# Relative-bias attention in a four-layer kernel: heads projected one by one and divided where they are added to X

## The reference

```
q, k, v = shape(h @ Wq), shape(h @ Wk), shape(h @ Wv)   # h: layernorm(x); 16 heads x 64
scores  = einsum('bhqd,bhkd->bhqk', q, k) + position_bias   # bias depends on k - q alone
attn    = softmax(scores, axis=-1)
out     = einsum('bhqk,bhkd->bhqd', attn, v)
x       = x + concat_heads(out) @ Wo
```

## Time and profile before

| | |
|---|---|
| median of 3 runs | 5371.87 us (5360.46 to 5372.24) |
| profiled execution, its own time | 5377.29 us |
| span of the profiled execution | 5375.2 us |
| busy in the span | TensorE 84%, weight loads 41%, VectorE 62%, ScalarE 50%, GpSimd 36% |
| mean granted TensorE clock | 0.931 |

### The profile page before, as it was taken

How to read it: one execution, slowest core, us unless ns; L and a number is a source line. 1 busy time by engine, 2 the same in 40 slices (tenths; PEclk the granted TensorE clock), 3 DMA queues, 4 the chain that set the end, 5 groups by cost and what they waited for, 6 DMA issues and landing times. The chain is left out here.

```text
span 5375.2 us, 70831 instructions
## 1 busy us (share of the span) xinstructions
PE 4499.2 (84%) x22404; PEld 2208.3 (41%) x22502; DVE 3330.0 (62%) x7491; ACT 2666.8 (50%) x4966; POOL 1911.9 (36%) x2206
## 2 busy tenths in 40 slices
PE   4678887988879888898888988798887888889888
PEld 2134334443444434443344433454334443445344
DVE  5766755667556674666655666556765667464445
ACT  2255553556526554365543745445553556436453
POOL 2746520555106541175301852036520555110200
PEclk8889998999989999999989999899998999999789
DMA  3523210332104211042100421023210332101000
GB/s 126 158 72 110 76 53 1 105 96 71 41 3 136 79 61 35 3 161 65 57 28 25 159 63 53 13 67 116 75 50 5 100 99 71 40 3 56 1 28 7
DMA packets 166645, 345.29 MB, mean 64 GB/s; under 512 B 18000, under 2 KB 26704, under 8 KB 166240
## 3 DMA queue, kind: packets, MB, share of 16 engines
q1 hardware_dynamic: 166256, 340.54, 19.9%
HBM read 337.25 MB, written 3.21 MB: 63 GB/s over the span
## 5 line engine op out<-in xcount | busy, mean ns | idle before, releaser
L196 PE MATMUL BANKS<-WB 128*128 128x512 bf16 x1518 | 440.1, 439 | 191.1 <-DVE XN L441 45.0
L1939 ACT ACTIVATE heads_prob<-BANKS 128x512 f32<-128x512 f32 (+3 forms) x768 | 365.3, 519 | 193.3 <-PE BANKS L1834 188.8
L407 POOL TENSOR_TENSOR rstd<-rstd,WF 128x4 f32<-128x4 f32 x48 | 48.5, 1011 | 944.7 <-DVE rstd L428 944.7
L1207 DVE CUSTOM_DVE_ANT_0 attn_biased<-BANKS,attn_toep 128x512 f32<-128x512 f32 x384 | 257.8, 682 | 188.3 <-PE BANKS L1095 134.1
L782 POOL TENSOR_TENSOR heads_work<-heads_work,heads_c_all 128x512 f32<-128x512 f32 x192 | 243.7, 1270 | 293.6 <-DVE heads_work L817 293.0
L196 PEld LDWEIGHTS BANKS<-WB 128*128 128x128 bf16 x1616 | 168.8, 110 | 422.8 <-issue 215.4
L212 POOL TENSOR_TENSOR rstd<-rstd,WF 128x4 f32<-128x4 f32 x24 | 24.3, 1011 | 787.5 <-DVE rstd L230 787.5
L1304 PEld LDWEIGHTS BANKS<-last_x_w,last_x_a 128*128 128x128 f32 x1536 | 214.7, 205 | 175.1 <-ACT last_x_a L1344 91.7
L1977 DVE CUSTOM_DVE_ANT_0 BANKS<-BANKS,WF 128x384 f32<-128x384 f32 (+3 forms) x512 | 241.2, 510 | 70.4 <-PE BANKS L1834 67.8
L1304 PE MATMUL BANKS<-last_x_w,last_x_a 128*128 128x128 f32 x1536 | 222.3, 291 | 71.0 <-ACT last_x_a L1344 71.0
L1980 DVE TENSOR_REDUCE heads_nmax<-BANKS 128x1 f32<-128x512 f32 x384 | 244.2, 682 | 60.1 <-PE BANKS L1834 59.0
(11 more groups left out here) (913 smaller groups left out, 10921.5 us busy)
## 6 DMA issues: line engine op xcount, KB each, us to landing
heads_c_all<-bc_rows SPq DMA_DIRECT2D x192, 256.0 KB, 3.2
attn_toep<-bias_line SPq DMA_DIRECT2D x96, 448.0 KB, 4.6
XNM<-bc_rows SPq DMA_DIRECT2D x112, 256.0 KB, 3.1
XTM<-bc_rows SPq DMA_DIRECT2D x112, 256.0 KB, 3.5
XO<-bc_rows SPq DMA_DIRECT2D x112, 256.0 KB, 3.3
XN<-bc_rows SPq DMA_DIRECT2D x112, 256.0 KB, 3.2
heads_b_all<-bc_rows SPq DMA_DIRECT2D x96, 256.0 KB, 3.6
last_x_w<-in_w SPq DMA_DIRECT2D x48, 512.0 KB, 3.7
```

Of the source, the lines that this page charges most:

```text
L196: nc.tensor.matmul(bank, ident_b, bc(ident_b[:, 0:1], [P, SEQ]), start=True, stop=True)
L1207: V.tensor_tensor_reduce(biased[:, s % NS_, :], PS[s % NS_], toep[:, h % 4, c:c + SEQ], -1.0, BIG, ALU.add, ALU.min, nmax[:, s:s + 1]).the ...
L1939: nc.scalar.activation(prob[:, i % PR, lo:hi], bank("T", i)[:, lo:hi], ACT.Exp).then_inc(exped, 1)
```

## The change

- The reciprocals are no longer spread by products. Bank 5 is copied as it is to `ot` (now by ScalarE), each head is projected by itself (64 rows of the array, two banks), and VectorE multiplies each 128 by 128 piece by the reciprocal of its row's sum as it adds it to X: eight instructions per pair, four for each head.
- Keys and values are reversed over the whole sequence (`XT` is written backwards by the norm), and queries are turned back; the bias line is reversed to match, and no reversal is left to undo.
- The ring has three banks, the scores have three in place of four. `biased` keeps four buffers, `prob` has six in place of five.
- The scores of a pair of steps are issued one step earlier, in the odd step.

```diff
-        NS_, NP_, NT_ = 4, 5, 2 * PAIR
-        RING = (PS[4], PS[7])
+        NS_, NB_, NP_, NT_ = 3, 4, 6, 2 * PAIR
+        RING = (PS[3], PS[4], PS[7])
+        NR = len(RING)
...
-            if spread_in(s) is not None:
-                order.append(("spread", spread_in(s)))
             if projected_in(s) is not None:
-                order.append(("project", projected_in(s)))
+                order += [("project", projected_in(s), 0), ("project", projected_in(s), 1)]
...
             def project(p):
-                bank = ring(("project", p))
+                halves = [ring(("project", p, a)) for a in range(2)]
                 pe.wait_ge(emptied, p + 1)
                 for j in range(NJ):
-                    last = nc.tensor.matmul(bank[:, j * D:(j + 1) * D], ot[:, p % 2, j * P:(j + 1) * P],
-                                            W("Wo")[:, p * D:(p + 1) * D], start=True, stop=True)
-                last.then_inc(filled, 1)
+                    for a in range(2):
+                        rows = slice(DK * a, DK * (a + 1))
+                        last = nc.tensor.matmul(halves[a][:, j * D:(j + 1) * D], ot[rows, p % 2, j * P:(j + 1) * P],
+                                                W("Wo")[rows, p * D:(p + 1) * D], start=True, stop=True)
+                        if j == NJ - 1:
+                            last.then_inc(filled, 1)
+
+            def score(s):
+                r, j = unit(s)[:2]
+                if s % PAIR == 0:
+                    pe.wait_ge(*freed(("make", r, 1)))
+                if s >= NS_ - 1:
+                    pe.wait_ge(maxed, s - NS_ + 2)
...
             make(0, 1)
+            score(0)
             for s in range(LAST):
                 r, rest = s // PAIR, s % PAIR
-                if s < U and s % 2 == 0:
+                if s + 1 < U and s % 2 == 1:
                     yield at(s)
...
+                    score(s + 1)
...
-                    nc.scalar.copy(dst if i else dst[:, :, ::-1],
-                                   bank.rearrange("p (j t) -> p j t", j=NJ)).then_inc(made, 1)
+                    dst = qk[:, r % 2, i, :]
+                    nc.scalar.copy(dst if i else dst[:, ::-1], bank).then_inc(made, 1)
...
+            def empty(w):
+                act.wait_ge(weighed, w + 1)
+                if w >= 2:
+                    act.wait_ge(filled, place["project", w - 2, 1] + 1)
+                nc.scalar.copy(ot[:, w % 2, :], PS[5]).then_inc(emptied, 1)
...
-            def add(p):
-                n = place["project", p]
+            def add(p, a):
+                n = place["project", p, a]
                 dve.wait_ge(filled, n + 1)
-                if p:
-                    dve.wait_ge(summed, p)
-                V.tensor_tensor(X[:, :, :], X[:, :, :], RING[n % 2].rearrange(tiles, j=NJ), ALU.add).then_inc(summed, 1)
...
+                if a == 0:
+                    dve.wait_ge(inverted, p + 1)
+                for j in range(NJ):
+                    done = PAIR * p + NJ * a + j
+                    if done >= NJ:
+                        dve.wait_ge(summed, done - NJ + 1)
+                    u = PAIR * p + 2 * j + a
+                    V.scalar_tensor_tensor(X[:, j, :], RING[n % NR][:, j * D:(j + 1) * D], rden[:, u:u + 1], X[:, j, :],
+                                           ALU.mult, ALU.add).then_inc(summed, 1)
...
-                    c = P * (NJ - 1 - j)
+                    c = P * j
...
-            norm_tiles(st, "ln", X, XN, XT, beside=await_weights)
+            norm_tiles(st, "ln", X, XN, XT[:, ::-1], beside=await_weights)
...
-    rel = np.arange(1024) - (SEQ - 1)
+    rel = (SEQ - 1) - np.arange(1024)
```

More of the change, by code:

```diff
@@ L955, in attn1_parts @@
             st.sem(n) for n in ("filled", "made", "copied_a", "copied_v", "scored", "maxed", "exped", "inverted"))
-        weighed, emptied, summed, spread = (st.sem(n) for n in ("weighed", "emptied", "summed", "spread"))
-        SPREAD_AT = 5
+        weighed, emptied, summed = (st.sem(n) for n in ("weighed", "emptied", "summed"))
         def at(s):
@@ L1011, in freed @@
             if item[0] == "project":
-                return summed, item[1] + 1
-            if item[0] == "spread":
-                return spread, item[1] + 1
+                return summed, PAIR * item[1] + NJ * (item[2] + 1)
             u = item[1]
@@ L1029, in ring @@
                 n = place[item]
-                if n >= 2:
-                    pe.wait_ge(*freed(order[n - 2]))
-                return RING[n % 2]
+                if n >= NR:
+                    pe.wait_ge(*freed(order[n - NR]))
+                return RING[n % NR]
             def make(r, i):
@@ L1045, in project @@
             def project(p):
-                bank = ring(("project", p))
+                halves = [ring(("project", p, a)) for a in range(2)]
                 pe.wait_ge(emptied, p + 1)
                 for j in range(NJ):
-                    last = nc.tensor.matmul(bank[:, j * D:(j + 1) * D], ot[:, p % 2, j * P:(j + 1) * P],
-                                            W("Wo")[:, p * D:(p + 1) * D], start=True, stop=True)
-                last.then_inc(filled, 1)
-            def spread_out(w):
-                bank = ring(("spread", w))
-                pe.wait_ge(inverted, w + 1)
-                for a in range(2):
[L1057 to L1062, removed]
+                    for a in range(2):
[10 more added lines that the diff above has]
+                    pe.wait_ge(maxed, s - NS_ + 2)
+                for a in range(2):
+                    o = DK * a
+                    q, k = qk[o:o + DK, r % 2, 0, :], qk[o:o + DK, r % 2, 1, :]
+                    nc.tensor.matmul(PS[(s + a) % NS_], q[:, j * P:(j + 1) * P], k,
+                                     start=True, stop=True).then_inc(scored, 1)
             def weigh(w, kt):
@@ L1129, in move @@
                 act.wait_ge(filled, n + 1)
-                bank = RING[n % 2]
+                bank = RING[n % NR]
                 if i == 2:
@@ L1135, in move @@
                 else:
-                    dst = qk[:, r % 2, i, :].rearrange("p (j t) -> p j t", j=NJ)
-                    nc.scalar.copy(dst if i else dst[:, :, ::-1],
-                                   bank.rearrange("p (j t) -> p j t", j=NJ)).then_inc(made, 1)
[L1140 to L1145, removed]
+                    dst = qk[:, r % 2, i, :]
[5 more added lines that the diff above has]
+                nc.scalar.copy(ot[:, w % 2, :], PS[5]).then_inc(emptied, 1)
             yield -2.0
@@ L1156, in scalar @@
                         act.wait_ge(filled, place["turn", e - NP_] + 1)
-                    nc.scalar.activation(prob[:, e % NP_, :], biased[:, e % NS_, :], ACT.Exp, bias=nmax[:, e:e + 1],
+                    nc.scalar.activation(prob[:, e % NP_, :], biased[:, e % NB_, :], ACT.Exp, bias=nmax[:, e:e + 1],
                                          scale=-1.0, accum_out=den[:, e:e + 1]).then_inc(exped, 1)
@@ L1165, in scalar @@
                         act.wait_ge(weighed, (u - NT_) // PAIR + 1)
[L1166 to L1169, removed]
+                    nc.scalar.copy(probt[:, u % NT_, :], RING[n % NR]).then_inc(copied_a, 1)
+                w = s // PAIR - 2
+                if s % PAIR == EMPTY_AT and 0 <= w < NPAIR:
+                    yield at(s) + 1.4
+                    empty(w)
                 if made_in(s):
@@ L1172, in scalar @@
                     move(*made_in(s))
+            yield at(LAST) + 1.0
+            empty(NPAIR - 1)
         def gpsimd(pool):
@@ L1220, in vector @@
                         dve.wait_ge(weighed, (u - NT_) // PAIR + 1)
[L1221 to L1225 removed]
+                    V.tensor_copy(probt[:, u % NT_, :], RING[n % NR]).then_inc(copied_v, 1)
                 if projected_in(s) is not None:
                     yield at(s) + 1.7
[L1228 to L1230 removed]
+                    add(projected_in(s), 0)
+                if s and projected_in(s - 1) is not None:
+                    yield at(s) + 1.7
+                    add(projected_in(s - 1), 1)
             yield at(LAST) + 3.0
[L1232 removed]
+            add(NPAIR - 1, 0)
+            add(NPAIR - 1, 1)
         pieces = Pieces()
```

44 lines of the change are left out of this document (5 added, 39 removed).

## The result

The changed kernel takes 5282.99 us (median of 3 runs, 5277.45 to 5286.52) against 5371.87; the ratio is 0.984, 95% interval 0.982 to 0.985. A second measurement of it gave 5274.68. So it is faster, by 89 to 98 us, where 128 were forecast. The profiled execution is the one of 5282.99 us.

A forecast was written before the change was run, and what follows sets the result against it. TensorE was taken as the bound, with 8.3 us of waits beside a scan. Seven scanning stages at -17.6 us give -123, the bare one -5: -128 from 5377.3, so 5249, in medians 5244; range 5195 to 5303, about 0.85.

The forecast's parts named there:

- Spread removed, shape changes: TensorE, per attention stage: removed spread saves 9.5 us, extra full/half-array changes from moved scores cost 4.7; sum -4.8.
- Projection by head: TensorE: sixteen 64-row products overlap in two halves and take 0.89 us again, so no net cost.
- The rival of no overlap: TensorE projections: the array halves don't overlap, 57 us of the gain go back, 5301 us; chance 0.04.
- Emptying to ScalarE, tail: ScalarE swaps one copy for another, even; a scanning stage's tail falls from 17.0 to 10.0 us, -7.0.
- Small additions: VectorE: eight 128-column additions at 0.26 us, +0.9 per pair; nothing in the middle, full price in the tail.
- the rival's 58 us: VectorE becomes the bound by its small additions: 58 us of the gain go back, 5302 us; chance 0.06.
- Third ring bank: Scanning stages: with the emptying off VectorE, aimed at 8.3 us of TensorE waits, of which 2.5 are kept.
- Three score banks, scores a step ahead: Scores hang on the maximum of the pair just ahead; priced at nothing beyond the waits kept.
- the slower rival: Each score waits for a maximum queued behind a scan; at 1.0 us per pair 5461 us; chance 0.06.
- The waits-stay rival: Queues of VectorE and GpSimd merely move TensorE's waits; gain 88 us, 5284 us; chance 0.20.
- GpSimd as a floor: GpSimd's scan work sets a floor near 127.5 us for a scanning stage before its tail.
- The first stage taken for all seven: Scanning stages: first stage's -10.6 and tail's -7.0 make -17.6, taken seven times for -123 us.

The follow-up runs named there:

- the third bank alone: Kernel before the change, with a third ring bank taken from the scores, which keep three banks; all else as before: 5340.46 us, ratio 0.994.
- the kernel with the scores back: Changed kernel with the scores issued in the even step again, ahead of its transposes: 5242.98 us, ratio 0.976.
- the two-bank kernel: Changed kernel with two ring banks in place of three, three score banks kept: 5335.11 us, ratio 0.994.
- the scan behind: Changed kernel with each scan queued behind the even step's maximum instead of ahead of it, scores still a step ahead: 5242.94 us, ratio 0.977.
- the kernel with the halves in turn: Changed kernel with a projection's products ordered head by head instead of alternating: 5287.35 us, ratio 0.984.
- the one that has only the pause put back: Changed kernel where the tail's first weighing also waits for the scan's last result (L925), emptying still on ScalarE: 5298.50 us, ratio 0.986.
- the eight-column sums: Changed kernel with scores in the even step, GpSimd's sums cut from 512 to 8 columns, result incomplete: 5220.07 us against 5242.98.
- the rows first: Changed kernel with scores in the even step, bias rows of heads 2 and 3 loaded behind the scan's first rows: 5227.86 us, ratio 0.973.
- the kernel with two decays: Changed kernel with the decay alternating between its bank and an SBUF buffer, five probability buffers instead of six: 5323.27 us, ratio 0.991.

## Why the prediction was right in sign and short in size

*Spread removed, shape changes.* Forecast -9.5 and +4.7 us per stage. The bare stage came out at 127.2 for 128.0, but partly by luck, for errors cancel in it. The third ring bank alone takes 2.7 us off it (132.8 to 130.1), where the forecast had nothing: it read 110.52 busy of 110.88 as a stage without waits. The same product of a `make` in the kernel before and in that with the third bank alone:

```profile
4893.45 1.02 PE L1037 MATMUL BANKS<-XT,WF 128*128 128x512 f32 x2
4894.51 0.66 PE L1103 MATMUL BANKS<-WF,zattn_prob 128*128 128x128 f32 x4
```

```profile
4871.18 1.02 PE L1038 MATMUL BANKS<-XT,WF 128*128 128x512 f32 x2
4872.03 0.60 PE L1104 MATMUL BANKS<-WF,zattn_prob 128*128 128x128 f32 x4
```

It occupies 1.06 us, and 0.85 with the third bank, and is busy for 1.02 in both: a wait this short hides behind the recorded duration. From there to the kernel with the scores back, 130.1 to 124.5, it is -5.6. By the starts of the products, the spread and the weighings ahead of it give -9.4, as forecast; the projections take +1.2 and the transposes +2.5, of which 1.3 is one wait for an addition; the forecast had both at nothing. The scores a step ahead then cost +2.7 (124.5 to 127.2) for a forecast 4.7: 2.1 is TensorE's busy time, 0.07 per excursion for 31 and not 0.15, and 0.6 is waits for maxima.

*Projection by head.* Forecast 0.89, measured 0.99:

```profile
420.26 1.16 PE L1041 MATMUL BANKS<-WF,attn_ot 64*128 64x128 f32 x16
421.25 1.03 PE L1055 MATMUL BANKS<-attn_qk 64*128 64x512 f32 x4
```

The rival of no overlap is out: undoing the alternation makes a projection of the bare stage 1.44 where it took 1.01.

*Emptying to ScalarE, tail.* Forecast 17.0 to 10.0, to the end of the last addition; measured, to the next norm, 10.2 from 16.1 to 17.4. The emptying back on VectorE brings the old tail back (15.6 to 17.2): shown.

*Small additions.* Forecast 0.26 us each and at nothing in the middle. VectorE's rows in the changed kernel:

```profile
421.45 1.13 DVE L1175 SCALAR_TENSOR_TENSOR X<-BANKS,attn_rden,X 128x128 f32<-128x128 f32 x4
422.50 0.68 DVE L1189 CUSTOM_DVE_ANT_0 attn_biased<-BANKS,attn_toep 128x512 f32<-128x512 f32 x1
423.10 1.12 DVE L1175 SCALAR_TENSOR_TENSOR X<-BANKS,attn_rden,X 128x128 f32<-128x128 f32 x4
```

Four take 1.05 us of queue (421.45 to 422.50), 0.26 each, where one operation on 512 columns takes 0.60 (422.50 to 423.10). The Trainium skill (VectorE: DVE Perf Modes, The TRN2 errata) says small pieces pay a latency each time; the rows agree. In the bare stage and in the first scanning stage alike 1.7 us of TensorE's waits are put down to L1175: small, and not the rival's 58 us.

*Third ring bank.* Forecast: keep 2.5 us of the waits for copies and banks. None were kept. Right in kind; the two-bank kernel shows that 60 us hang on it, twice what the bank is worth on the kernel before (5372 to 5340), because the change itself makes the ring busier. The emptying off VectorE, which the forecast counted beside it, did nothing in the middle.

*Three score banks, scores a step ahead: the step that failed.* It was priced at nothing beyond the waits kept. It brings 6.4 us of waits for maxima in the first stage, 3.7 with the scores back and 1.5 with the scan behind; the scan's place alone takes 30 us off the kernel's attention. The mechanism had been named as the slower rival and set aside, because the maximum and the score need less than half of the 4.0 us between two scores. That compared their work with the interval, and left out the scan of 1.2 us ahead of them and the scan's own wait for its decay (up to 1.5 us). The maximum comes late in six of 31 pairs of steps, so the price was 0.2 us per pair and not the rival's 1.0. It did not show in the stage's sum, 135.4 for 134.4, because the forecast had kept 6.4 us of other waits (2.5 and 3.9), most of which went: two errors that nearly cancel. The waits-stay rival names 5284, where the time fell, and it said that the queues would move the waits. But it let a scanning stage gain 4.8 us, where 9.0 were measured, and its sign, waits ahead of transposes for copies, did not come; its sum agrees because of the microseconds outside attention.

*GpSimd as a floor.* Forecast 127.5 per stage. The best kernels stand at 129.5, and the sums' removal takes only 2 us off: near it, not on it.

*The first stage taken for all seven.* Attention fell by 114.8 us and not by 128. The step multiplied the first stage's numbers by seven: its tail of before was 17.4 us to the next norm, the others' 16.1 to 16.5, so the tails gave 6.3 on the mean and not 7.0; and the stages gave 9.0 and not 10.6, the seventh of after being 137.9. The last sequence gave 7.5 and not 5: 5.6 before its tail, and 1.8 ahead of its first scores, where the profiled execution before had a granted clock of 0.64 for 9.5 us and that of after 1.00 for 7.7.

*Outside attention: no step at all.* The other 26 us of the 39 that the forecast is short of 5282.99 lie here (rest 4035.8 before, 4061.7 after; 4054.4 in the second measurement). The same stretches behind the fifth attention, before and after:

```profile
3108.00:3123.60 15.60, 12.17 (x62) 8.28 (x65) 9.20 (x37) 1.25 (x4) 1.02 (x1) 0.89 0.00 1
3123.60:3215.30 91.70, 77.45 (x473) 30.53 (x476) 67.62 (x193) 58.51 (x124) 58.20 (x116) 0.98 0.29 84
```

```profile
3038.20:3054.00 15.80, 11.73 (x62) 7.19 (x65) 9.24 (x37) 1.26 (x4) 1.02 (x1) 0.85 0.00 1
3054.00:3147.10 93.10, 79.51 (x473) 31.46 (x476) 67.62 (x194) 58.63 (x124) 58.08 (x116) 0.95 0.26 83
```

The work is the same; the granted clock is 0.89 and 0.98 here with a pause of TensorE ahead, 0.85 and 0.95 without one. It need not be the pause, though. The same place in the kernel with the halves in turn, which has no pause:

```profile
3042.10:3058.60 16.50, 13.08 (x64) 7.58 (x65) 9.23 (x37) 1.25 (x4) 1.02 (x1) 0.82 0.00 1
3058.60:3148.90 90.30, 76.53 (x475) 30.50 (x476) 67.58 (x194) 58.52 (x124) 57.96 (x116) 1.00 0.27 85
```

Over the seven scanning sequences the two stretches sum to 754.9 us before and 769.6 after, but also to 753.6 in this kernel and 754.0 with two ring banks, both without the pause, and to 759.2 in the one that has only the pause put back. Two kernels put the pause back with the change otherwise in place, and both have their rest, by medians, at 4041, against 4050 to 4062 in most kernels without it. But the third bank on the kernel before has the pause and 4048.2, the eight-column sums have none and 4043.6, and one kernel repeats only within 7, or within 15 in its profiled executions. What costs the 19 to 26 us outside attention stays open; the runs show that the granted clock there changes with the kernel and the execution.

## What to carry to other kernels

When a wait is taken from one consumer of a busy in-order queue, ask who is next behind the same long instruction. Here the copies were freed of the scan and the scores tied to it; compare the chain in front of the new wait, the long instruction and its own wait included, with the slack, not the work alone. Nor does a busy share near 100% say that an engine never waits: on an engine at 110.52 of 110.88 us a third bank still found 2.7. Of two cures for one wait try each alone first: the scores back in their place and the scan moved gave over 30 us each, and with the rows first the second on top of the first gave nothing (5234 for 5228). The fastest kernel here that computes the whole result has the scores back in the even step and the scan's rows loaded first, 5228 us, 2.7% under the kernel before.

## What the runs showed of the hardware

A scan with both inputs in SBUF and a GpSimd product that reads SBUF shut each other out. VectorE and GpSimd in the kernel with two decays:

```profile
377.00 2.10 DVE L920 TENSOR_TENSOR_SCAN attn_e_work<-attn_e_decay,attn_e_work 128x512 f32<-128x512 f32 x1
...
385.65 1.23 DVE L920 TENSOR_TENSOR_SCAN attn_e_work<-attn_e_decay,attn_e_work 128x512 f32<-128x512 f32 x1 [1.72 <-ACT attn_e_decay L885]
```

```profile
376.75 1.27 POOL L893 TENSOR_TENSOR attn_e_work<-XNM,m_du 128x512 f32<-128x512 f32 x1
...
385.90 2.05 POOL L893 TENSOR_TENSOR attn_e_work<-XNM,m_du 128x512 f32<-128x512 f32 x1
```

At 377.00 the product has begun first, and the scan takes 2.10 us: it ends 1.08 behind the product's end (378.02). At 385.65 the scan is first, takes 1.23, and the product takes 2.05. With the decay in a bank the scans take 1.22 beside the same products. The Trainium skill (SBUF — State Buffer, SBUF: two separate sides) says that a VectorE operation with two SBUF inputs and a GpSimd operation that reads SBUF hold a shared pair of ports for a whole instruction, and that whichever starts first blocks the other; these rows agree. In the kernels before and after, the one product beside L925, which also has two inputs in SBUF, takes 1.79 us in each of the seven stages, where others take 1.27: the same thing at a small price.
